# A graph-attention layer on one core: edge steps in every third turn instead of every second, dense rows in half blocks with a shorter chain per four of them, and six groups' senders fetched by edge number

## The reference, cut to what matters

```
edge_feat = concat(x[rcv], x[snd], edge_attr_3, edge_weight1)        # 25000 x 260
h1 = silu(edge_feat @ W1 + b1);  h2 = silu(h1 @ W2 + b2);  score = h2 @ W3 + b3
alpha = softmax of score over the edges of one receiver
msg = (x[snd] @ Wv) * alpha * node_vec[snd]
out = layernorm(x + x + sum of msg over the edges of one receiver)   # every one of the 100000 rows
```

## Time and profile before

| | us |
|---|---|
| median of 3 runs | 1098.7 (1092.56 to 1099.37) |
| profiled execution, its own time | 1094.48 |
| span of that execution, first to last instruction | 1092.7 |
| busy: PE / DVE / ACT / POOL | 799.0 / 733.9 / 511.8 / 573.6 |
| mean granted TensorE clock | 0.876 of full |
| HBM read and written | 111.41 MB and 77.76 MB |

### The profile page before, as it was taken

How to read it: one execution, slowest core, us unless ns; L and a number is a source line. 1 busy time by engine, 2 the same in 40 slices (tenths; PEclk the granted TensorE clock), 3 DMA queues, 4 the chain that set the end, 5 groups by cost and what they waited for, 6 DMA issues and landing times.

```text
span 1092.7 us, 14171 instructions
## 1 busy us (share of the span) xinstructions
PE 799.0 (73%) x3908; PEld 527.4 (48%) x3908; DVE 733.9 (67%) x2804; ACT 511.8 (47%) x1181; POOL 573.6 (52%) x600
## 2 busy tenths in 40 slices
PE   0001776778888878887888888889999999998600
PEld 0000444444555545555555555556667666766500
DVE  8988777666767776677777777786443544537741
ACT  0000345444444545454554455556765666665540
POOL 2002765655555655555562223323777777646677
PEclk9999878788888988898898888989999999999755
DMA  4001677877777867776787567764643333321231
GB/s 122 0 0 40 193 249 251 265 243 248 274 243 243 275 222 248 245 262 221 247 265 250 181 227 243 253 208 140 179 97 97 106 98 98 94 78 60 67 79 46
DMA packets 106357, 189.99 MB, mean 174 GB/s; under 512 B 18907, under 2 KB 77942, under 8 KB 93736
## 3 DMA queue, kind: packets, MB, share of 16 engines
q1 hardware_dynamic: 87400, 150.42, 42.0%
q0 software_dynamic: 18880, 38.68, 12.3%
HBM read 111.41 MB, written 77.76 MB: 173 GB/s over the span
## 4 chain that ended last, share of the span: by engine, by line
PE 62%; DVE 20%; issue 6%; DMA 6%; POOL 4%; SPq 1%; ACT 1%; DVEq 0%; POOLq 0%; ACTq 0%
PE bank L662 29%; DVE hk L926 7%; DMA region<-rec_d 5%; PE bank L607 4%; PE bank L651 4%; PE bank L644 4%; POOL out_rows L423 4%; PE bank L625 4%; PE bank L600 4%; PE bank L622 3%; PE bank L623 3%; PE bank L585 2%; DVE region L712 2%; DVE region L713 2%; DVE xin L907 2%
## 5 line engine op out<-in xcount | busy, mean ns | idle before, releaser
L477 ACT ACTIVATE xin<-xin,drs 128x128 f32<-128x128 f32 x637 | 254.1, 480 | 310.0 <-DVE drs L877 310.0
L662 PE MATMUL bank<-hk 128*125 128x512 bf16 x1176 | 330.8, 449 | 63.9 <-DVE snd_i L940 60.1
L419 POOL DMA_INDIRECT rec<-in_xw,snd_i x196 | 185.3, 946 | 283.7 <-DMA rec_d<-rec 192.5
L662 PEld LDWEIGHTS bank<-hk 128*125 128x125 bf16 x1176 | 188.9, 164 | 188.9 <-issue 128.1
L419 POOL DMA_INDIRECT hk<-in_x,kg_t x196 | 186.6, 952 | 143.6 <-DVE kg_t L796 84.2
L423 POOL DMA_INDIRECT out_rows<-hk,sidx_t x196 | 191.8, 979 | 82.5 <-issue 56.7
L892 DVE BATCH_NORM_STATS2 dst<-xin 128x6 f32<-128x256 f32 x392 | 134.9, 409 | 0.1
L933 DVE SCALAR_TENSOR_TENSOR hk<-hk,cid,bank 125x512 f32<-125x512 f16 x49 | 36.6, 747 | 137.8 <-PE bank L662 137.8
L926 DVE TENSOR_SCALAR hk<-hk,rid 128x512 bf16<-128x512 f16 x392 | 116.5, 368 | 0.1
L985 DVE TENSOR_TENSOR hk<-bank,hk 128x512 f32<-128x512 f32 x49 | 33.6, 685 | 80.7 <-PE bank L644 80.7
L529 ACT ACTIVATE hk<-hk,ers 128x128 f32<-128x128 f32 x196 | 79.6, 482 | 0.8 <-DVE ers L877 0.8
(11 more groups left out here) (187 smaller groups left out, 1095.8 us busy)
## 6 DMA issues: line engine op xcount, KB each, us to landing
xin<-in_x SPq DMA_DIRECT2D x49, 1024.0 KB, 4.9
out_rows<-xin SPq DMA_DIRECT2D x49, 1024.0 KB, 6.1
rec_d<-rec SPq DMA_DIRECT2D x49, 258.0 KB, 4.9
region<-rec_d SPq DMA_DIRECT2D x49, 258.0 KB, 4.3
hk<-vc_d SPq DMA_DIRECT2D x49, 256.0 KB, 3.7
krow<-seg_d SPq DMA_DIRECT2D x49, 128.0 KB, 3.6
hk<-in_x,kg_t POOLq DMA_INDIRECT x196, 4.1
rec<-in_xw,snd_i POOLq DMA_INDIRECT x196
```

Source lines behind the costliest of these rows:

```text
L419: pool.indirect_dma_start(out=to, out_offset=None, in_=frm, in_offset=bass.IndirectOffsetOnAxis(ap=index, axis=0)).then_inc(done, 16)
L477: ins = nc.scalar.activation(xin[:, j % X_RING, n, :], xin[:, j % X_RING, n, :], ACT.Identity, bias=drs[:, j % 2, 1, n:n + 1], scale=drs[: ...
L662: ins = pe.matmul(bank[7][0:SEL, :], tab[:, k, n, 0:SEL], oh[:, k, :], start=(k == 0 and n == 0), stop=(k == CH - 1 and n == PIECES - 1))
```

## The change

1. **Steps in thirds of the turns.** `turn_plan` puts whole steps (three parts, all in one turn) into every third turn from turn 10, and into each turn from turn 43. There are then 99 turns instead of 95.
2. **43 lookups instead of 49.** Groups 4, 12, 20, 28, 36 and 44 (`TAKEN`) are not searched. The host lays the five words of each edge out by edge number (`rec5`), and POOL fetches them with 24 gathers of 128 rows of 5 words (`rt`), issued behind the first 16 receiver gathers. DVE copies them out in turn 7 (12 small copies). Getting the edge numbers as row indices costs two small DVE instructions, two PE transposes and a copy in the preparation.
3. **The search may start early.** DVE makes three one-hot tables, copies the words of the last lookup, then makes the other five; PE's search starts on the first three. Before, all eight and the dense rows came ahead of the copies.
4. **Dense rows in half blocks.** 98 blocks of 8 rows per partition (512 KB), two a turn, in a ring of 8 (the same memory). ACT takes 7 of 8 rows, DVE 1. The chain has 11 instructions instead of 13 and runs once per four half blocks (twice as wide, every second turn). The scaling follows the statistics by two turns instead of one. ACT's rows of a turn stand ahead of the step's work (7 rows) and behind it (7 rows); before, they stood in three pieces between it.
5. **Lags.** The senders' write is 7 turns behind the lookup instead of 5 (`REC_LAG`), the receiver gathers lead by 4 groups instead of 5 (`LEAD`).

```diff
-BR = 16
+BR = 8
-HS_RING, R_RING, X_RING = 4, 12, 4
+HS_RING, R_RING, X_RING = 4, 12, 8
-ACT_ROWS = 13
+ACT_ROWS = 7
-LEAD = 5
-REC_LAG = 5
-E_FROM = 8
+LEAD = 4
+REC_LAG = 7
+E_FROM = 10
+PARTS = 3
+FIRST_TAKEN, TAKEN_STEP = 4, 8
+TAKEN = tuple(range(FIRST_TAKEN, G, TAKEN_STEP))
+LOOKED = tuple(g for g in range(G) if g not in TAKEN)
+EARLY = 3
-STEPS = 13
+STEPS = 11
...
 def pool_plan():
-    order = [("hk", g) for g in range(LEAD)]
+    order = [("hk", g) for g in range(LEAD)] + [("rt", k) for k in range(len(TAKEN))]
     for g in range(G):
         order.append(("hs", g))
         if g + LEAD < HK_LOW:
...
-            for i, s in enumerate(TURNS):
-                if i + 1 < G:
+            for i, now in enumerate(TURNS):
+                store_block(2 * (i - 3) + 1)
+                if i + 1 < LOOKS:
                     load_places(i + 1)
-                if 0 <= i - REC_LAG < G:
-                    write_rec(i - REC_LAG)
+                for g in range(G):
+                    if looks(g) - 1 + REC_LAG == i:
+                        write_rec(g)
...
-                dense(i)
+                if i >= 3:
+                    load_block(2 * (i + 1))
+                store_block(2 * (i - 2))
+                if i >= 3:
+                    load_block(2 * (i + 1) + 1)
...
+                elif kind == "rt":
+                    if g == 0:
+                        pool.wait_ge(S["tab_ready"], 1)
+                    for q in range(TPG):
+                        t = TAKEN[g] * TPG + q
+                        gather(rt[:, g, q, :], rec5, idx_t[:, t:t + 1], S["rt_in"])
...
+            for i, now in enumerate(TURNS):
+                norm(i, 0)
+                for s, part in now:
+                    (turned, hidden, results)[part](s)
+                norm(i, 1)
...
+            def look(u):
+                if u < LOOKS:
+                    wait(pe, "pay_ready", u)
                     for k in range(CH):
+                        if k == 0:
+                            wait(pe, "oh_ready", 2 * u + 1)
+                        elif k == EARLY:
+                            wait(pe, "oh_ready", 2 * u + 2)
                         for n in range(PIECES):
...
+            for i, now in enumerate(TURNS):
+                if 0 <= i - 1 < LOOKS:
+                    take_places(i - 1)
+                one_hot(i, 0, EARLY)
+                for b in range(NBATCH):
+                    if (batch_end(b) + 4, 0) in now:
+                        take_scores(b)
+                if 0 <= i - 1 < LOOKS:
+                    take_words(i - 1)
+                one_hot(i, EARLY, CH)
+                if i == REC_LAG:
+                    take_gathered()
+                dense_norm(i)
+                for s, part in now:
+                    (part_one, part_two, part_three)[part](s)
+                dense_stats(i)
+                more(99)
```

More of the change, by code:

```diff
@@ L66, in turn_plan @@
 def turn_plan():
[L68 to L74, removed]
+    plan, left, turn = [], [(s, p) for s in range(LAST_STEP) for p in range(PARTS)], 0
+    while left:
+        now = []
+        if turn >= LOOKS or (turn >= E_FROM and (turn - E_FROM) % PARTS == 0):
+            now.append(left.pop(0))
+            while left and left[0][0] == now[0][0]:
+                now.append(left.pop(0))
+        plan.append(now)
         turn += 1
@@ L79, with looks @@
 TURNS = turn_plan()
+def looks(g):
+    return sum(1 for v in LOOKED if v <= g)
 def pool_plan():
-    order = [("hk", g) for g in range(LEAD)]
+    order = [("hk", g) for g in range(LEAD)] + [("rt", k) for k in range(len(TAKEN))]
     for g in range(G):
@@ L381, in _ @@
                         load_far(b)
-                if s is not None:
+                for s, part in now:
+                    if part > 0:
+                        continue
                     if s + 1 < G:
@@ L561, in _ @@
             pe.wait_ge(S["flip_ready"], 7)
+            for h in range(2):
+                pe.transpose(bank[7][:, h * SROWS:(h + 1) * SROWS], row["neg"][0:SROWS, h * P:(h + 1) * P], ident[0:SROWS, 0:SROWS])
             for k, name in enumerate(("sidx", "seg")):
@@ new lines, in scores @@
+            def scores(s):
+                g = s - 3
+                if 0 <= g < G:
+                    b, last = batch_of(g), g == batch_end(batch_of(g))
+                    wait(pe, "x2_ready", g + 1)
+                    wait(pe, "s_taken", b)
+                    for q in range(TPG):
+                        n = (g % BATCH) * TPG + q
+                        ins = pe.matmul(bank[3][0:BT, 0:P], wz[:, BT - 1 - n:2 * BT - 1 - n], x2[:, q * P:(q + 1) * P],
+                                        start=(n == 0), stop=(last and q == TPG - 1), skip_group_check=True)
+                    ins.then_inc(S["score_done"], 1)
@@ new lines, in second, with first @@
+            def second(s):
+                g = s - 2
+                if 0 <= g < G:
+                    wait(pe, "x1_ready", g + 1)
+                    wait(pe, "x2_ready", g)
+                    pe.matmul(bank[2][:], w2s[:], x1[:], start=True, stop=True).then_inc(S["mm2_done"], 1)
+            def first(s):
+                g = s - 1
+                if 0 <= g < G:
+                    wait(pe, "hkT_ready", g + 1)
+                    wait(pe, "hsT_ready", g + 1)
+                    wait(pe, "efT_ready", g + 1)
+                    wait(pe, "x1_ready", g)
+                    pe.matmul(bank[1][:], w1a[:], hkT[:, g % 2, :], start=True, stop=False, skip_group_check=True)
+                    pe.matmul(bank[1][:], w1b[:], hsT[:, g % 2, :], start=False, stop=False, skip_group_check=True)
+                    for q in range(TPG):
+                        ins = pe.matmul(bank[1][:, q * P:(q + 1) * P], w16[:, q, :], efT[:, g % 2, :],
+                                        start=False, stop=(q == TPG - 1), skip_group_check=True)
+                    ins.then_inc(S["mm1_done"], 1)
@@ L610, in _, with turns, words @@
+            def turns(s):
+                if s + 1 < G:
+                    turn_rows(s + 1)
+                    turn_senders(s + 1, sum(batch_end(b) + 5 <= s for b in range(NBATCH)))
+            def words(u):
+                if 0 <= u < LOOKS:
                     wait(pe, "sel_ready", u + 1)
@@ L664, in _ @@
                     ins.then_inc(S["found"], 1)
+            for i, now in enumerate(TURNS):
+                if i == E_FROM:
+                    turn_rows(0)
+                    turn_senders(0, 0)
+                for s, part in now:
+                    (scores, first, sums)[part](s)
+                    if (s, part) == now[0]:
+                        words(i - 1)
+                    (second, small_turns, turns)[part](s)
+                if not now:
+                    words(i - 1)
+                look(i)
             pe.wait_ge(S["fix_in"], 16 * 11)
```

327 lines of the change are left out of this document (157 added, 170 removed).

## The result

| | before | changed |
|---|---|---|
| median of the runs of the comparison, us | 1095.6 | 1037.5 (1035.08 to 1045.32) |
| ratio, 95% interval | 1 | 0.948 (0.9415 to 0.955) |
| span of the profiled execution | 1092.7 | 1033.3 |
| forecast | | 1005, range 982 to 1050 |

A forecast was written before the change was run, and what follows sets the result against it. A loop through several engines, no single one, was taken to bound the kernel. First search at 109.1, lookups over at 566.0, lone steps to 905.7 and tail 95.3 made span 1001.0; run-time allowances gave 1005 us, range 982 to 1050.

The forecast's parts named there:

- the 5 us for POOL: Lookup stage: search 37 put at 508, against 503.2 by the turns alone and 503.9 by POOL's gathers.
- the gap of 2.25 us: Plain lookup turn: PE's time from search end to next search falls from 4.03 to 2.25 us.
- A plain turn of 9.3: Lookup turn without a step: 9.3 us, chosen between 8.4 at full clock and 10.5.
- A step turn of 14.3, then 15.5: Lookup turn with a step: search 5.3 plus 8.63 and some second senders' writes, 14.3 us; 15.5 from step 10 on.
- The two limits: Start of search 37: 503.2 by the sum of turns, 503.9 by POOL's gathers, said to fall within 1 us.
- Half blocks bounded by 258 KB and 1 MB rows: DMA: unseen 512 KB store and load landings taken to lie between 4.3 and 4.9, and 4.9 and 6.1 us.
- the ring's cover: Half-block buffers: store and load need 11.5 us of 15.0 available, 3.5 us to spare.
- Crowded DMA: Rival, chance 0.22: full DMA queues make plain turns 10.5 and step turns 16 us, total 1050, from 1025 to 1085.
- The overhang of 15 us behind the lookups: Turns 43 to 50: ACT's dense rows delay PE's wait for hsT, 15 us in all, bounds 0 and 25.
- Lone steps at 8.30: Steps after the last search: 8.30 us each, 39 steps from step 11 to 50, 323.7 us.
- the tail of 95.3: After step 50: drain, scatters and the fix to the end, unchanged at 95.3 us.

The follow-up runs named there:

- the load ahead: The changed kernel with the senders' load of a step issued at the end of the SP turn before; ratio 0.930 to the kernel before, 20 us faster than the changed kernel.
- ACT's order: The changed kernel with ACT making hkT, hsT and x2 ahead of its dense rows from turn 43 on; ratio 0.932 to the kernel before.
- both repairs: The changed kernel with the senders' load one turn ahead and ACT's copies ahead of its dense rows after the lookups; ratio 0.916 to the kernel before, 1000.3 us.

## Why the prediction was right or wrong

- *The point and the range*: 1037.5 lies within 982 to 1050, but outside the 985 to 1025 that the prediction called its own forecast. The range reached that far for the crowded queues, whose plain turns of 10.5 did not come. And terms that were too dear (plain turns by 9 us in all, the 5 us for POOL, the lone steps by 5) hid part of those that were too cheap (the step turns by 29, the overhang by 18). That the total lies within the range is in part luck.
- *What bounded the kernel before, and the gap of 2.25 us*: right. Measured 2.23 to 2.24 in most plain turns, 2.5 on average; the early copies are worth 40 us alone and 44 when undone, 70% of the gain or more.
- *A plain turn of 9.3*: 9.0 over 31 turns, alternating between 7.6 and 9.3 as foreseen. Only the reason is another. It was put to DVE's chain in every second turn; but with a chain in each turn the 7.6 us turns were still there from turn 17 on. In PE's rows the 9.3 us turns are those with a search of 7.08, partly at the lower clock, and the time between searches is 2.23 in both kinds: no chain is waited for. The clock did follow the shorter gap where there are no steps yet: 0.82 before, 0.91 now. In the stage with steps it stayed at 0.87 (0.86 before).
- *A step turn of 14.3, then 15.5*: the term that failed, in two places. It was 20.0 in turn 10 and 16.8 over the ten from turn 13. First, the load: its 5.94 us were taken over from the earlier trace rows although two terms of the same sum made the queue fuller; it took 9.84 in turn 10 and 6.2 to 8.6 behind it, and it stands on SP behind the places, one or two writes and, now, a store. The time between two searches came to 9.9 where the sum had 9.0 in nine of these ten turns. Issuing the load earlier gave back 20 us. Second, and the larger part in these ten turns, the search: the sum counts it at 5.3, full clock, while the earlier trace rows, from which it takes the rest, shows 8.25, and in the kernel before the searches ahead of a step took 7.5 on average. It measured 6.9, so 1.5 us a turn more. None of the variants was aimed at that; with the load ahead it is 6.9 still.
- *POOL*: the timing was right within 3.5 us (senders of group 34 forecast from 488.1, measured 491.6; no pause longer than a spacing from 99.97 to 511). That it binds was wrong for the changed kernel: SP waited for no gather. It was right for the kernel without the late load (51.6 and 95.3 us of such waits). The two limits were not 1 us apart but 20, because the other was mis-sized.
- *Half blocks bounded by 258 KB and 1 MB rows*: wrong. 7.3 and 6.9 us lie above both ends: with the share at 0.90 these landings are not bounded by size. By these medians the ring's cover was 0.3 us (0.5 + 6.9 + 7.3 against 15.0), not 3.5. It still sufficed; DVE waited 2.0 us for x in all.
- *Crowded DMA at 0.22*: neither the case nor excluded. It predicted its mark of 1050 through longer plain turns as well; these were not longer, and a sixth of the stage's bytes less gave 3 us. Its other term, step turns of 16 since their load waits in the same queues, came nearer to the 16.8 than the forecast's 14.3. The queue's order is what showed. The Trainium skill's HBM figure (DMA: Bandwidth & Descriptors, Specifications), about 358 GB/s per core, would have put a plain turn at 9.1 us on average at best, an estimate from that figure. But the Trainium skill says on the same page (Bandwidth, Measured) that this is what each core gets with both cores of a pair streaming, and this kernel runs on one; the prediction left that out. 9.0 us was measured with less than the forecast's bytes in some turns, and the fullest stage, with the load ahead, moved 301 GB/s at a share of 0.93. Of the stretches read here only the two us of the earlier trace rows lie above the figure, so as a mean it is neither borne out nor refuted.
- *The overhang of 15 us behind the lookups*: the mechanism was right and shown (14.4 us by ACT's order), the size was 33. 18 of the 33 lie in the two softmax turns (19.6 and 17.1 us, where one behind the dense rows takes 9.5), in which DVE's statistics now stand behind ACT's exponential; the change moved them there, and the sum did not price it. Putting them back took 4.4 us off the ten turns. With ACT's order alone 19 us are still over the lone steps, and no run takes all of that apart.
- *Lone steps at 8.30 and the tail of 95.3*: 8.12 and 95.1.
- *Ratio*: both repairs give 0.916; the forecast was 1005 / 1098.7 = 0.915. The two waits are most of what the forecast missed, but so close an agreement is luck: with both repairs searches 0 to 10 took 92.9 us (forecast 98.0), a plain turn 8.8 (9.3), a step turn from turn 13 on 15.8 (14.3, then 15.5) and steps 11 to 21 101.1 (98), and the differences cancel.

## What to carry to other kernels

When a change makes a shared queue fuller, re-price every latency on the critical path that passes through it, and look at what stands ahead of that one transfer: moving it one turn forward was worth 20 us here, cutting a sixth of the stage's bytes 3. Take each term of a sum from a row of its own kind: the searches ahead of steps ran at 7.5 us in the kernel before, and counting them at 5.3 cost more of the forecast in ten turns than the load did. Work that is moved to the end of a turn for the sake of the next stage hangs behind every wait of that turn, so price it in the turn with the longest wait, not in the mean one. Try the cheapest part alone first: three tables, two copies, then five tables gave 40 of 57 us without any of the other parts.

## What the runs showed of the hardware that was not expected

- The granted clock followed the shorter idle time only in part: in the turns ahead of the first step it rose from 0.82 to 0.91, in the stage with steps from 0.86 to 0.87. Searches partly at the lower level (6.1 to 7.9 us instead of 5.4) still stand in 21 of the 31 plain turns, with 2.23 us between searches in most.
- 512 KB transfers landed in 7.3 us at a DMA share of 0.90, where 1 MB took 4.9 at 0.73; with the DMA share nearly idle again (0.29) the senders' load fell to 2.8 us.
- POOL's gathers kept their spacing of 1.25 us throughout, with DVE at its fullest and at a DMA share of 0.93 (10.0 us for the eight gathers of a group); only their landing rose, from 4.1 to 5.7 us for the receivers' rows.
